# Two pairs of weight buffers and moved 32x32 blocks in a graph-attention kernel

## What is computed

```python
type_sum = adj @ x
attn_a = sigmoid(concat([type_sum, x], axis=1) @ Wa.T + ba)
attn_b = sigmoid(concat([type_sum, x], axis=1) @ Wb.T + bb)
h = x @ W_sa
s_left, s_right = h @ a_sa[0, :512], h @ a_sa[0, 512:]
scores = s_left[:, None] + s_right[None, :]
e = where(adj != 0, exp(-leaky_relu(scores, 0.01)), 0.0)
attn = e / (sum(e, axis=1) + 1e-5)
x_a = attn @ h
x_b = adj @ (x @ W_gcnb) + b_gcnb
return layernorm(x + sigmoid(attn_a * x_a + attn_b * x_b))
```

## Time and profile before

| what | value |
| --- | --- |
| time, median of 3 runs | 956.04 us (955.63 to 956.14) |
| the profiled execution | 955.64 us |
| its span, first to last instruction | 953.8 us |
| TensorE clock granted, mean | 0.999 of full |
| busy: TensorE / VectorE / ScalarE / GpSimd | 942.8 / 672.4 / 356.3 / 198.5 us |
| mean transfer rate | 114 GB/s |

### The profile page before, as it was taken

How to read it: one execution, slowest core, us unless ns; L and a number is a source line. 1 busy time by engine, 2 the same in 40 slices (tenths; PEclk the granted TensorE clock), 3 DMA queues, 4 the chain that set the end, 5 groups by cost and what they waited for, 6 DMA issues and landing times.

```text
span 953.8 us, 12642 instructions
## 1 busy us (share of the span) xinstructions
PE 942.8 (99%) x4368; PEld 783.6 (82%) x4368; DVE 672.4 (70%) x1264; ACT 356.3 (37%) x618; POOL 198.5 (21%) x508
## 2 busy tenths in 40 slices
PE   9999999999999999999999999999999999999996
PEld 6888887788888888888888888888888888898885
DVE  6988868976676676676676576577577576476758
ACT  4555445432433333333343343243343243343322
POOL 3111100211211221221221221221221221222132
PEclk9999999999999999999999999999999999999999
DMA  9789632345433435433435434435433334343321
GB/s 283 193 195 229 175 108 78 88 106 105 113 103 94 121 95 113 112 96 100 117 94 116 111 94 105 111 94 116 111 95 105 111 94 94 89 111 95 95 62 44
DMA packets 139551, 108.97 MB, mean 114 GB/s; under 512 B 10336, under 2 KB 113632, under 8 KB 139488
## 3 DMA queue, kind: packets, MB, share of 16 engines
q1 hardware_dynamic: 102720, 62.42, 22.3%
q0 software_dynamic: 35904, 44.31, 21.5%
q10 hardware_dynamic: 864, 1.44, 0.8%
HBM read 101.32 MB, written 6.83 MB: 113 GB/s over the span
## 4 chain that ended last, share of the span: by engine, by line
PE 93%; DVE 3%; issue 2%; POOL 1%; ACT 1%; DVEq 0%; POOLq 0%; ACTq 0%
PE bank L570 15%; PE bank L572 15%; PE bank L571 15%; PE bank L595 13%; PE bank L596 13%; PE bank L619 4%; PE bank L620 4%; PE bank L621 4%; PE bank L581 2%; PE bank L582 2%; PE bank L614 1%; PE bank L553 1%; POOL scratch L331 1%; DVE product L713 1%; PE bank L607 0%
## 5 line engine op out<-in xcount | busy, mean ns | idle before, releaser
L570 PE MATMUL bank<-e_hi,x_hi 128*128 128x512 f32 (+1 forms) x728 | 273.2, 375 | 1.4 <-DVE e_lo L749 1.1
L572 PE MATMUL bank<-e_lo,x_hi 128*128 128x512 f32 (+1 forms) x728 | 272.4, 374 | 0.0
L571 PE MATMUL bank<-e_hi,x_lo 128*128 128x512 f32 (+1 forms) x728 | 272.3, 374 | 0.0
L391 ACT ACTIVATE e_hi<-u,c_col 128x512 fp32r<-128x512 f32 (+1 forms) x182 | 126.1, 693 | 328.5 <-DVE u L737 217.5
L344 POOL DMA_DIRECT2D adj_r<-adj_t_dram x180 | 103.7, 577 | 660.9 <-PE bank L596 545.6
L595 PE MATMUL bank<-x_hi,adj_r 128*128 128x512 f32 x572 | 224.9, 393 | 0.0
L596 PE MATMUL bank<-x_lo,adj_r 128*128 128x512 f32 x572 | 223.0, 390 | 0.0
L749 DVE SCALAR_TENSOR_TENSOR e_lo<-u,c_col,e_hi 128x512 fp32r<-128x512 f32 (+1 forms) x182 | 129.9, 714 | 50.8 <-ACT e_hi L391 41.5
L570 PEld LDWEIGHTS bank<-e_hi,x_hi 128*128 128x128 f32 x728 | 137.0, 188 | 27.4 <-DVE e_lo L749 1.9
L571 PEld LDWEIGHTS bank<-e_hi,x_lo 128*128 128x128 f32 x728 | 137.0, 188 | 24.9
L572 PEld LDWEIGHTS bank<-e_lo,x_hi 128*128 128x128 f32 x728 | 137.0, 188 | 24.6
(11 more groups left out here) (119 smaller groups left out, 839.2 us busy)
## 6 DMA issues: line engine op xcount, KB each, us to landing
adj_r<-adj_t_dram POOLq DMA_DIRECT2D x158, 256.0 KB, 3.1
adj<-adj_t_dram SPq DMA_DIRECT2D x156, 256.0 KB, 3.1
out_dram<-y SPq DMA_DIRECT2D x24, 256.0 KB, 3.8
z1s<-x_dram SPq DMA_DIRECT2D x14, 256.0 KB, 6.0
adj<-adj_t_dram SPq DMA_DIRECT2D x26, 128.0 KB, 2.4
adj_r<-adj_t_dram POOLq DMA_DIRECT2D x22, 128.0 KB, 2.6
z2s<-x_dram SPq DMA_DIRECT2D x6, 256.0 KB, 8.3
y<-x_dram SPq DMA_DIRECT2D x6, 256.0 KB, 5.3
```

Of the source, the lines that this page charges most:

```text
L391: nc.scalar.activation(e_hi[g % E_RING][:, 0:cols(b)], u[g % U_RING][:, 0:cols(b)], ACT.Copy, scale=c_col[:, j:j + 1]).then_inc(e_hi_ready, 1)
L570: nc.tensor.matmul(z1[k][:, 0:n], x_hi[:, j, kk], e_hi[s][:, 0:n], start=(j == 0), stop=False)
L571: nc.tensor.matmul(z1[k][:, 0:n], x_lo[:, j, kk], e_hi[s][:, 0:n], start=False, stop=False)
L572: ins = nc.tensor.matmul(z1[k][:, 0:n], x_hi[:, j, kk], e_lo[s][:, 0:n], start=False, stop=(j == TILES - 1))
```

## The change

- `e_hi` and `e_lo` have two buffers each instead of three (`E_RING`), and `adj_r` has three instead of four (`ADJ_R_RING`).
- For tiles 0 to 23 TensorE no longer turns z2. VectorE transposes `z2s` within 32x32 blocks into `turned_blocks` (`turn_blocks`, at i = 0 behind `z2_lo(t-1)`), and SyncE moves the blocks to their places in `z2t` with 16 transfers from SBUF to SBUF, each of 32 partitions x 4 x 128 bytes (`move_blocks`, at i = 1 behind `load_adj`). `z2_hi` and `z2_lo` read `z2t` instead of the bank. The last two tiles are turned as before.
- `l_row` has two buffers. `load_l(b)` waits for the exponentials of block b-2 instead of b-1; the first of them is issued at j = 12 instead of 24.
- The last tile's z2 parts lie in `adj_r` instead of `e_hi[2]` and `e_lo[2]`.

```diff
-E_RING = 3
+E_RING = 2
-ADJ_R_RING = 4
+ADJ_R_RING = 3
...
+        z2t = sb("z2t", [P, KT, P])
+        l_row = [sb(f"l_row{s}", [P, WIDE * P]) for s in range(2)]
+        turned_blocks = sb("turned_blocks", [P, D])
...
+        z2_blocks = turned_blocks[:, :].rearrange("p (k m i) -> p k m i", k=KT, m=4)
...
+        MOVES = 16 * 16
...
+            def move_blocks(t):
+                sp.wait_ge(blocks_turned, t + 1)
+                since(sp, zt_lo_ready, 2 * t)
+                for a in range(4):
+                    for m in range(4):
+                        sp.dma_start(z2t[32 * m:32 * m + 32, :, 32 * a:32 * a + 32],
+                                     z2_blocks[32 * a:32 * a + 32, :, m, :]).then_inc(z2_moved, 16)
...
+                if i == 1:
+                    move_blocks(t)
...
             def load_l(b):
-                act.wait_ge(exp_done, TILES * b)
+                since(act, exp_done, TILES * (b - 1))
...
             def copy_z2(n):
                 act.wait_ge(adj_r_used, sums_done(n))
-                since(act, turn_done, n - 1)
+                if n >= 2:
+                    act.wait_ge(blocks_turned, n - 1)
...
             def z2_hi(t):
-                act.wait_ge(turn_done, t + 1)
+                act.wait_ge(z2_moved, MOVES * (t + 1))
                 act.wait_ge(proj_done, 2 * t + 1)
-                nc.scalar.copy(zt_hi[:, :, :].rearrange("p k i -> p (k i)"), turned[:, :]).then_inc(zt_hi_ready, 1)
+                nc.scalar.copy(zt_hi[:, :, :], z2t[:, :, :]).then_inc(zt_hi_ready, 1)
...
+                if j == 12:
+                    load_l(1)
                 if j == TILES - 2:
-                    load_l(1)
                     row_factor(0)
...
             for b, q, t, i, j, chunks in places():
-                if i == 0:
-                    since(pe, zt_lo_ready, 2 * t)
-                    turn(t, turned)
-                    if q == 0 and b > 1:
-                        pe.wait_ge(denoms, b)
+                if i == 0 and q == 0 and b > 1:
+                    pe.wait_ge(denoms, b)
...
+            def turn_blocks(t):
+                dve.wait_ge(z2_copied, t + 1)
+                since(dve, z2_moved, MOVES * t)
+                nc.vector.transpose(turned_blocks[:, :], z2s[:, t % 2, :]).then_inc(blocks_turned, 1)
...
                 if i == 0:
                     if t >= 1:
                         z2_lo(t - 1)
+                    turn_blocks(t)
                     if q == 0:
                         denominators(b - 1)
```

More of the change, by code:

```diff
@@ L116, in adj_resnorm_kernel @@
         adj_r = [sb(f"adj_r{s}", [P, CHUNK, P], F32R) for s in range(ADJ_R_RING)]
-        l_row = sb("l_row", [P, WIDE * P])
+        z2t = sb("z2t", [P, KT, P])
+        l_row = [sb(f"l_row{s}", [P, WIDE * P]) for s in range(2)]
+        turned_blocks = sb("turned_blocks", [P, D])
         esum = sb("esum", [P, WIDE * P])
@@ L149, in adj_resnorm_kernel @@
         w_t = [w_gate[:, k // 2, k % 2, :] for k in range(KT)]
-        a_wide = [t[:, :].rearrange("p (k m) -> p k m", k=KT) for t in (l_row, esum)]
+        a_wide = [t[:, :].rearrange("p (k m) -> p k m", k=KT) for t in (l_row[0], esum)]
+        z2_blocks = turned_blocks[:, :].rearrange("p (k m i) -> p k m i", k=KT, m=4)
         diag = x_row[:, :].rearrange("p (q i) -> p q i", q=WIDE)
@@ L180, in adj_resnorm_kernel @@
             sem(n) for n in ("row_up_ready", "den_ready", "denoms", "inverses", "alpha_ready"))
+        blocks_turned, z2_moved = sem("blocks_turned"), sem("z2_moved")
         turn_done, zt_hi_ready, zt_lo_ready, proj_done = (
@@ L382, in steep @@
                 since(act, e_lo_ready, g - U_RING + 1)
-                nc.scalar.activation(u[g % U_RING][:, 0:cols(b)], l_row[:, 0:cols(b)], ACT.Exp,
+                nc.scalar.activation(u[g % U_RING][:, 0:cols(b)], l_row[b % 2][:, 0:cols(b)], ACT.Exp,
                                      bias=r_col[:, j:j + 1]).then_inc(exp_done, 1)
@@ L394, in load_l @@
             def load_l(b):
-                act.wait_ge(exp_done, TILES * b)
+                since(act, exp_done, TILES * (b - 1))
                 act.wait_ge(l_saved, 16 * b)
-                nc.scalar.dma_start(l_row[:, 0:cols(b)],
+                nc.scalar.dma_start(l_row[b % 2][:, 0:cols(b)],
                                     l_dram[b:b + 1, 0:width(b)].rearrange("b q p -> b (q p)")
@@ L468, in _ @@
             act.wait_ge(l_spread, WIDE)
-            nc.scalar.copy(l_row[:, :], z1[0][:, :]).then_inc(l_first, 1)
+            nc.scalar.copy(l_row[0][:, :], z1[0][:, :]).then_inc(l_first, 1)
             source_factor(0)
@@ L521, in _ @@
             gate_exps(LAST - 1)
-            act.wait_ge(turn_done, LAST)
+            act.wait_ge(turn_done, 1)
             act.wait_ge(proj_done, 2 * (LAST - 2) + 2)
@@ L533, in _ @@
             copy_z2(LAST)
-            act.wait_ge(turn_done, LAST + 1)
-            nc.scalar.copy(e_hi[2][:, :], z2[0][:, :]).then_inc(zt_hi_ready, 1)
+            act.wait_ge(turn_done, 2)
+            nc.scalar.copy(adj_r[0][:, :, :].rearrange("p k i -> p (k i)"), z2[0][:, :]).then_inc(zt_hi_ready, 1)
             gate_exps(LAST)
@@ L700, in _ @@
             for n, half in enumerate(HALVES):
-                project(1, lambda k: e_hi[2][:, k * P:(k + 1) * P], lambda k: e_lo[2][:, k * P:(k + 1) * P], last_p2[n],
+                project(1, lambda k: adj_r[0][:, k, :], lambda k: adj_r[1][:, k, :], last_p2[n],
                         half=half)
@@ L805, in z1_lo @@
                                         ALU.subtract).then_inc(zt_lo_ready, 1)
+            def turn_blocks(t):
+                dve.wait_ge(z2_copied, t + 1)
+                since(dve, z2_moved, MOVES * t)
+                nc.vector.transpose(turned_blocks[:, :], z2s[:, t % 2, :]).then_inc(blocks_turned, 1)
             def z2_lo(t):
                 dve.wait_ge(zt_hi_ready, 2 * t + 2)
-                nc.vector.tensor_tensor(zt_lo[:, :, :].rearrange("p k i -> p (k i)"), turned[:, :],
-                                        zt_hi[:, :, :].rearrange("p k i -> p (k i)").bitcast(F32),
+                nc.vector.tensor_tensor(zt_lo[:, :, :], z2t[:, :, :], zt_hi[:, :, :].bitcast(F32),
                                         ALU.subtract).then_inc(zt_lo_ready, 1)
@@ L983, in _ @@
             dve.wait_ge(zt_hi_ready, 2 * LAST)
-            nc.vector.tensor_tensor(e_lo[2][:, :], z2[0][:, :], e_hi[2][:, :].bitcast(F32), ALU.subtract) \
+            nc.vector.tensor_tensor(adj_r[1][:, :, :].rearrange("p k i -> p (k i)"), z2[0][:, :],
+                                    adj_r[0][:, :, :].rearrange("p k i -> p (k i)").bitcast(F32), ALU.subtract) \
                 .then_inc(zt_lo_ready, 1)
```

## The result

The changed kernel takes 996.13 us (994.9 to 997.68, 4 runs) where the kernel before takes 956.09 (955.63 to 956.34, 4 runs) beside it: ratio 1.042, interval 1.0407 to 1.0434. The forecast was 949, the range 945 to 960. The profiled execution took 997.68 us with a span of 995.9 and a mean TensorE clock of 0.973 of full; before, 0.999.

What follows compares the result with a forecast made beforehand. TensorE, busy 942.8 of 953.8 us, was taken to bound the kernel. From 955.64, less 10.1 for turns, plus 1.4 for the opening and 1.6 for the adjacency ring, gives 948.5; on the median 948.9, say 949; range 945 to 960.

Steps and rivals of the forecast that it cites:

- Added on SyncE: 16 transfers a tile at 0.46 us an issue, 7.4 us; adjacency loads and store(t-2) wait behind; hidden.
- the limit, 0.95: On SyncE, the moves were to stay hidden until one issue costs 0.95 us.
- Two weight buffers instead of three ... 3.3 us to spare: e_hi waits for step g-2; e_lo(112) still ends 3.3 us before TensorE wants it; steady state costs nothing, but thin.
- both in the same lead, nothing: z2's copy and rest reading SBUF, and load_l a block earlier, lie in VectorE's lead over TensorE: no cost.
- The turns: On TensorE, turns cost 0.48 us a tile; removing them saves 10.1 us over 21 tiles from t = 3 on.
- The opening: Tiles t = 0 to 2, turns included: net +1.4 us, from 0 to +5; step 38 ends 3.0 us late.
- The adjacency ring: Three adjacency buffers instead of four: chunk 3's load late at the start, +1.6 us (0 to 3); hidden in steady state.
- The transpose: On VectorE, 128x512 in 32x32 blocks: 0.6 us once a tile, far bound 2.2, covered by VectorE's lead.
- The packets: The moves' 2048 packets of 128 bytes a tile: 2 us of each DMA engine, hidden in a 35 us tile.
- The small transfers hold up the other queues: Rival: adj_r loads land late beside the moves, TensorE waits 1.6 us after about 10 six-step quarters: 965; chance 0.18.
- The Trainium skill's advice to turn blocks on TensorE: Against moving 128x128 turns off TensorE; if the replacement ate the whole gain, 959; chance 0.02.
- the rings cost more: Rival: slow transpose adds 2 x 1.6 us in the opening, or thin places open: 951.5 to 958; chance 0.18.

Runs made afterwards that it cites:

- E2: The kernel before with two pairs of weight buffers instead of three, last tile's z2 parts in adj_r, no moves: 978.27 us.
- E8: The changed kernel with three pairs of weight buffers, the gates' x half left out for room, moves and late l_rows write kept: 958.99 us.
- E9: The changed kernel with three pairs of weight buffers, the gates' x half left out, and the l_rows write a tile earlier: 945.71 us.
- E7: The kernel before with two pairs of weight buffers and the l_rows write a tile earlier, no moves: 960.56 us.
- E1: The changed kernel with the l_rows write at i = 4 of a block's third tile instead of i = 3 of its fourth: 948.91 us.
- E4: The kernel before with three adj_r buffers instead of four, nothing else: 956.31 us.
- E3: The changed kernel with the fourth tile's 16 moves issued behind the l_rows write instead of ahead of it: 967.03 us.

## Why the prediction failed

**The step that failed** is in "Added on SyncE": "Behind them wait the adjacency loads from i = 2 on and store(t-2)." A third kind of issue waits there, the write of `l_rows` in each block's fourth tile. It is the last of them and the only one with little slack: its data need 9.2 us to land, and the old kernel issued it 7.7 us before `load_l` waits for it. That wait's row could be had from the old trace (the line below); I looked up the write's landing and took it only as a price for small packets. The wrong size beside it, 0.64 us an issue where I took 0.46 (10.8 us in block 2's fourth tile, not 7.4), made it worse; by the point that I gave as the limit, 0.95, it should have been harmless.

```profile
ACT e_hi L391 <- DMA l_rows<-l_col: 2.8, 1, 2.8
```

**"Two weight buffers instead of three ... 3.3 us to spare"** was checked for one reader alone, TensorE at `e_lo`, and that held: there is no wait for `e_lo` after the opening. But a lead that shrinks by a step also shrinks for what hangs on the masks elsewhere. SyncE's queue goes by the masks, and ScalarE's `load_l` by the projections on TensorE. The 4.4 us between the two were not in the sum. For load_l I had written "both in the same lead, nothing", and looked only at the buffer that it fills, not at the row that it reads. E2 shows this step alone at 17.7 us, E8 against E9 the one above alone (with the slower landing) at 13.3.

**The half clock** was in no term and no rival: 17 of the 49.6 us. I had priced each stall at its own length.

**What was right.** The turns: 0.48 a tile, met at each tile but the last two (0.41); with three weight buffers and the early write the exchange brings 10.2 us (E9 under the kernel before, the gates' x half left out), and 11.7 with two (E7 against E1), 2.6 of them being E7's two late turns. The opening: 2.1 - 0.55 = 1.5 us, forecast 1.4, and by the path forecast: 0.7 late at step 26 (0.76) and 3.2 at step 38 (3.0), though in three stalls for `e_lo` instead of one. The adjacency ring: the other 0.55, forecast 1.6, in its range; E4 finds it alone within the noise. The transpose: 0.70 us, 0.6 taken, never waited for. The packets: q1's share rose from 22.3% of 953.8 us to 26.6% of 995.9, that is by 52 us of each engine or 2.2 a tile, where I took 2. The moves land in 2.3 us, and the adjacency loads in 3.2 instead of 3.1.

**The rivals.** "The small transfers hold up the other queues" ended on the right side for the wrong reason: its mechanism, TensorE waiting for a late adj_r load in the six-step quarters, happened nowhere, and E1, with every one of its transfers, takes 949. The rule of the Trainium skill that spoke for it (DMA: Bandwidth & Descriptors, section Specifications: below 512 bytes no full rate, but read, modify and write) decided nothing here. The moves did take 2.2 us of each engine a tile, where in proportion to bytes it would be 0.9; but they landed in 2.3 us, and no engine waited for them. The Trainium skill's advice to turn blocks on TensorE (VectorE: DVE Perf Modes, section Rules for kernel authors) is also decided by the runs: on a TensorE that is full, leaving it pays 10.2 us (E9) or more, once the write is out of the way. The rival "the rings cost more" came by neither of its ways: the transpose took 0.70 us, and in E1 all of TensorE's waits for `e_lo` and `z1s` lie in the opening. What two buffers cost as such, 3.2 us by E1 against E9, lies there too (2.7 of it), where the sum had its 1.4.

That the forecast's 949 is what E1 measures shows that the sum of the parts that I named was sound, and the list of the parts was not. That the two agree within 0.1 us is luck: the adjacency ring alone was put 1.0 us too dear.

## What to carry to other kernels

When transfers are put into an issuing engine's list, write down everything that stands behind them in that list over a whole block, the rare entries too, with the time from each one's issue to the moment its reader waits. The rare entry, once a block, had 7.7 us against some 8.5 needed, while the frequent ones had plenty. When a ring is made shorter, ask of every engine that follows the ring's pace what it issues for an engine that doesn't. And a new stall of TensorE should be priced with the slower clock behind it: here stalls of 4.8 to 9.5 us cost another 2.5 to 3.7 us each, about half as much again in total.

## What the runs showed of the hardware

- An issue from SyncE of one 32 x 4 x 128 byte transfer within SBUF took 0.60 us, and sixteen of them 10.2 to 11.6 in the changed kernel; loads of 256 KB took 0.37 when alone, and 0.46 in a row of four.
- After each of the five stalls of 4.8 to 9.5 us TensorE was granted 1.2 GHz, until 5.2 to 7.8 us after it had resumed. Shorter stalls went both ways: in E8 those of 1.2 and 1.5 us (blocks 2 and 3) were followed by 3.4 us at 1.2 GHz, one of 2.1 us in E2 (block 3) and those of 0.8 us in E3 and E8 (block 5) were not.
- A write of 2 KB in 512 pieces of 4 bytes let its reader go 8.0 to 10.05 us after its issue in the kernel before, 10.2 to 11.7 in E8, with two loads and a store of 256 KB issued in the 1.7 us ahead of it, and 7.0 to 11.4 in E2, with one load. What delays it was not tried apart.
- E8 scatters over 1.2% where the others keep within 0.4%: ScalarE's waits there, 4.4 to 7.2 us in the profiled execution, lie close to TensorE's 3.65 us of cover. That this is why it scatters is argued, not shown.
